# Moving three groups of SBUF tiles by 64 bytes in a four-layer graph network kernel

## What is computed

```python
h = relu(layernorm(x)); x = x + elu(softmax(where(adj > 0.5, leaky_relu(Wh1 + Wh2.T), -9e15), axis=1) @ (h @ W0))
h = relu(layernorm(x)); x = x + relu(D @ (adj + I) @ D @ h @ W1 + bias)      # D = diag(rsqrt(rowsum(adj + I)))
h = relu(layernorm(x)); x = x + relu(adj @ h @ W2) * row_mask
h = relu(layernorm(x)); x = x + relu(h @ Wa + ((adj @ h) / rowsum(adj)) @ Wb)
```

## The kernel before

| tiles | start modulo 512, before | after |
|---|---|---|
| w_hi, w_lo | 128 | 128 |
| v_rows, bias_rows, ident | 0 | 64 |
| xs, a_raw, a_hi, a_lo | 64 | 128 |
| a_rows, a_diag | 384 | 448 |
| h, h_hi, h_lo | 384 | 448 |
| t_hi, t_lo, ht_hi, ht_lo | 384 | 384 |
| z, act_out, scores, mask_add | 384 | 384 |
| p_hi, p_lo | 64 | 128 |

## Time and profile before

### The profile page before, as it was taken

How to read it: one execution, slowest core, us unless ns; L and a number is a source line. 1 busy time by engine, 2 the same in 40 slices (tenths; PEclk the granted TensorE clock), 3 DMA queues, 4 the chain that set the end, 5 groups by cost and what they waited for, 6 DMA issues and landing times.

```text
span 2565.7 us, 40515 instructions
## 1 busy us (share of the span) xinstructions
PE 2491.4 (97%) x13216; PEld 2151.6 (84%) x13216; DVE 2000.7 (78%) x4373; ACT 1398.7 (55%) x2571; POOL 1212.0 (47%) x1607
## 2 busy tenths in 40 slices
PE   2799999999999999999999999999999999999998
PEld 2688888888888888888888888888888888888887
DVE  6787887877877878788787787787787788788853
ACT  3555555555555555555555555556555555555542
POOL 2454545545544544544544544544544545445431
PEclk8899999999999999999999999999999999999999
DMA  4112122122122121122121221221221221221110
GB/s 143 42 38 59 50 58 58 47 61 56 49 62 51 53 62 50 55 62 49 55 62 48 56 62 48 57 62 47 57 62 46 59 62 45 59 63 45 43 34 25
DMA packets 338321, 141.35 MB, mean 55 GB/s; under 512 B 269760, under 2 KB 302528, under 8 KB 338112
## 3 DMA queue, kind: packets, MB, share of 16 engines
q1 hardware_dynamic: 338112, 138.75, 20.2%
HBM read 73.14 MB, written 33.55 MB: 42 GB/s over the span
## 4 chain that ended last, share of the span: by engine, by line
PE 95%; DVE 1%; issue 1%; POOL 1%; ACT 1%; SPq 0%; DMA 0%; POOLq 0%; ACTq 0%; DVEq 0%
PE O L314 46%; PE T L314 35%; PE X L314 13%; PE X L335 1%; POOL h_lo L802 0%; SPq L276 0%; ACT h L442 0%; DMA act_out<-w_all 0%; POOL xs L767 0%; DVE ht_lo L654 0%; DVE p_lo L633 0%; DVE scores L566 0%; DVE w_lo L556 0%; DVE ln_stats L584 0%; POOL ln_scale L788 0%
## 5 line engine op out<-in xcount | busy, mean ns | idle before, releaser
L802 POOL TENSOR_TENSOR h_lo<-h,h_hi 128x512 fp32r<-128x512 f32 x384 | 534.3, 1413 | 354.4 <-ACT h_hi L448 354.4
L442 ACT ACTIVATE h<-xs,ln_bias,ln_scale 128x512 f32<-128x512 f32 x512 | 396.0, 811 | 423.6 <-POOL ln_bias L796 423.6
L314 PE MATMUL O<-w_hi,t_hi 128*128 128x512 f32 x1536 | 597.8, 389 | 0.0
L314 PE MATMUL O<-w_lo,t_hi 128*128 128x512 f32 x1536 | 597.5, 389 | 0.0
L314 PE MATMUL O<-w_hi,t_lo 128*128 128x512 f32 x1536 | 597.5, 389 | 0.0
L639 DVE TENSOR_TENSOR t_lo<-T,t_hi 128x512 fp32r<-128x512 f32 x512 | 347.6, 689 | 297.1 <-ACT t_hi L454 297.1
L454 ACT CAST t_hi<-T 128x512 fp32r<-128x512 f32 x512 | 298.1, 583 | 417.7 <-PE T L314 417.7
L767 POOL TENSOR_TENSOR xs<-xs,act_out 128x512 f32<-128x512 f32 x128 | 164.0, 1300 | 591.1 <-ACT act_out L481 556.1
L584 DVE BATCH_NORM_STATS2 ln_stats<-xs 128x6 f32<-128x512 f32 x512 | 327.3, 679 | 18.3 <-POOL xs L773 12.5
L314 PEld LDWEIGHTS O<-w_hi,t_lo 128*128 128x128 f32 x1536 | 288.3, 188 | 59.8
L314 PEld LDWEIGHTS O<-w_hi,t_hi 128*128 128x128 f32 x1536 | 288.3, 188 | 55.3 <-DVE t_lo L639 0.5
(11 more groups left out here) (95 smaller groups left out, 5061.9 us busy)
## 6 DMA issues: line engine op xcount, KB each, us to landing
xs<-x SPq DMA_DIRECT2D x64, 512.0 KB, 3.6
out<-xs SPq DMA_DIRECT2D x64, 512.0 KB, 3.0
h<-act_out SPq DMA_DIRECT2D x976, 32.0 KB, 1.9
a_raw<-adj_t SPq DMA_DIRECT2D x64, 256.0 KB, 2.7
a_rows<-adj SPq DMA_DIRECT2D x64, 256.0 KB, 2.7
xs<-w_all SPq DMA_DIRECT2D x6, 512.0 KB, 6.9
act_out<-w_all SPq DMA_DIRECT2D x2, 512.0 KB, 6.6
z<-w_all SPq DMA_DIRECT2D x2, 512.0 KB, 6.4
```

The lines of the kernel that those rows point to most:

```text
L314: last = nc.tensor.matmul(psum, s, m, start=(start and n == 0 and i == 0), stop=(stop and n == len(pairs) - 1 and i == 2))
L442: nc.scalar.activation(h[:, k.odd, m], xs[:, k.xb, m], ACT.Relu, bias=ln_bias[:, k.quad, m:m + 1], scale=ln_scale[:, k.quad, m:m + 1], acc ...
L802: nc.gpsimd.tensor_tensor(h_lo[:, k.odd, m], h[:, k.odd, m], h_hi[:, k.odd, m].bitcast(F32), ALU.subtract).then_inc(h_lo_ready, 1)
```

## The change

A new tile `t_distance` of 448 bytes per partition is put ahead of t_hi, and the two unused tiles that exist grow by 64 bytes each. Everything from v_rows to h_lo lies 64 bytes further on, everything from t_hi to mask_add 512 bytes, and everything from p_hi on 576 bytes. The weights stay. Nothing reads or writes the three unused tiles, and no instruction of any engine differs but for its addresses.

```diff
-        distance = sb("distance", [P, 96])
+        distance = sb("distance", [P, 112])
...
         h_lo = sb("h_lo", [P, 2, NT, F], F32R)
+        t_distance = sb("t_distance", [P, 112])
         t_hi = sb("t_hi", [P, 2, FT, N], F32R)
...
-        p_distance = sb("p_distance", [P, 48])
+        p_distance = sb("p_distance", [P, 64])
         p_hi = sb("p_hi", [P, NT, N], F32R)
```

## The result

| | before | after |
|---|---|---|
| median of 20 runs each, us | 2567.18 | 2571.31 |
| lowest and highest | 2566.54, 2569.35 | 2569.17, 2572.74 |
| the profiled execution, us | 2567.61 | 2572.03 |
| its span, us | 2565.7 | 2570.2 |

After takes 1.0014 of the time before, interval [1.0008, 1.002]; the medians are 4.1 us apart. The forecast was 2565.0, a little less than before. The median lies inside the range 2546 to 2588, but the sign is the other one. The difference is under the 0.2% that the chances were set for, and yet its interval leaves out 1.

A forecast was written before the change was run, and what follows sets the result against it. The prediction took TensorE's matmul steps to bound the kernel; with only `gather_last` gaining 1.9 us and all else 0, 2566.7 became 2564.8, said as 2565.0 us, range 2546 to 2588.

The forecast's parts named there:

- What bounds the kernel: Steady part, about 2350 of 2566 us: TensorE always busy, so time is the number of matmuls times their step.
- Projections, 0 us: Matmuls with weights moving and t or ht loaded, 120 of 204 per period: offsets modulo 512 unchanged, so 0 us.
- Gathers, 0 us: 4608 matmuls of 256 columns: difference stays 320, step stays 117.6 ns; bounds 19.8 us less to 27.6 us more.
- The reading that the difference decides, and not the place: In the gathers: loaded less moving offset sets the step, so an unchanged difference of 320 costs 0 us.
- `gather_last`, 1.9 us less: 768 matmuls, t moving and a loaded: step falls from 229.2 to 226.7 ns; bounds nothing or 4.6 us.
- Edges between groups, 0 us with a bound of 1: Last matmul ahead of a gather, h loaded beside it: some 190 at 5 ns, under 1 us, taken as 0.
- Other engines and DMA, 0 us: Other engines not later, DMAs of `carry` hidden though their share might rise to at most twice 0.32; 0 us.
- The ht_lo that had 0.2 us in hand: Layer 3's turned h on VectorE: lateness might cost up to 12 us, expected 0; 0.23 together with the slower rival.
- Nothing happens: First rival: TensorE never waits on anyone, no address matters, 2566.7 us; chance 0.12.
- The boundary: Second rival: operands off a multiple of 128 bytes cost, not the difference; 2556.5 us, chance 0.27 with its variant.
- The third, slower one: Loaded operand 64 bytes past a multiple of 128 costs 2.5 to 6 ns per gather matmul; 0.23 with late ht_lo.
- the second rival's variant: Gathers all run at the start-up's 113.3 ns, 19.8 us less, 1.9 lost behind; 2547 us, within the rival's 0.27.

The follow-up runs named there:

- e3: Every tile 64 bytes further on than in the kernel before, weights and t included, so all differences stay; 1.0002 [0.9993, 1.0012] of its time.
- e8: Against the kernel before, a and p moved to offset 0 and h to 320 modulo 512, weights and t kept; 0.9989 [0.9978, 1.0001].
- e9: Against the kernel before, a and p moved to offset 192 and h to 256 modulo 512, weights and t kept; 1.0014 [1.0004, 1.0024].
- e12: The placement of e8 again with more rounds (a and p at 0, h at 320 modulo 512), against the kernel before; 0.9989 [0.998, 0.9998].
- e1: Against the kernel before, only the graph matrices a and the attention p moved 64 bytes on, h and t kept; 1.004 [1.0025, 1.0055].
- e4: Against the kernel before, a and p moved 128 bytes on and h 64, modulo 512, weights and t kept; 1.0068 [1.0053, 1.0083], 2585.5 us.
- e5: Against the kernel before, a moved to offset 0 and p to 448 modulo 512, the rest kept; 1.0058 [1.0035, 1.0081].
- e7: Against the kernel before, a moved to offset 256 and p to 192 modulo 512, the rest kept; 1.0051 [1.0029, 1.0074].
- e13: Against the kernel before, a and p moved to offset 0 and h to 224 modulo 512, weights and t kept; 1.0009 [0.9999, 1.0019], 2570.0 us.
- e11: Against the kernel before, a moved to offset 224 and p to 160 modulo 512, the rest kept; 1.0056 [1.0036, 1.0076].
- e14: Against the kernel before, a and p moved to offset 96 and h to 160 modulo 512, weights and t kept; 1.0058 [1.0039, 1.0076].
- e10: Against the kernel before, a moved to offset 32 and p to 96 modulo 512, the rest kept; 1.0046 [1.003, 1.0062].

## Why the prediction was wrong

**What bounds the kernel: right.** TensorE is busy for all of each period in after too, the waits are empty, and in the steady part the whole difference is matmuls that start later one after the other.

**Projections, 0 us: right within the group, wrong at its start.** From the sixth matmul on the step is 226.7 ns as before.

**Gathers, 0 us: right.** Extra 107 before and after. The reading that the difference decides, and not the place, is what e3 shows.

**`gather_last`, 1.9 us less: right.** 27.5 to 0 ns a graph is 1.8 us less for 64 graphs.

**Edges between groups, 0 us with a bound of 1: this is the step that failed.** It looked at one kind of edge only, the one that leads into a gather (weights or t moving, h loaded), and took for its price the 5 ns by which one slow step differs from a fast one. The edge that costs is the one out of a gather, and it costs five steps and not one: 27.5 ns, 3 x 64 = 192 times, 5.3 us. The forecast lies 6.3 us under the result: 5.3 are these edges, and 0.4 the median of before, 2567.18 over 20 runs for the 2566.74 that the forecast started from. The prediction had a row of that very kind before it and read it as small: in the start-up three projections behind a fast gather take 0.69 us where three take 0.68 elsewhere. It priced them at 0.01 us and let them occur only where the gathers ran fast. From that row it should have kept a term of 0.01 us for each of 192 edges, and by the rounding of both times up to 0.02, in the forecast itself: 1.9 to 3.8 us more, which takes away the gain of `gather_last` or turns the sign. That would still be under the 27.5 ns of each edge; no row that it shows has that size.

**Other engines and DMA, 0 us: right.** The ht_lo that had 0.2 us in hand never made TensorE wait. The DMA share of a period is 0.21 and 0.20 against 0.22 and 0.21, so that pieces crossing more boundaries, if they cost anything, stay hidden.

**The rivals.** "Nothing happens" is refuted by `gather_last` and the projections, which went opposite ways; that their sum is small is chance. The boundary is refuted by e3. The third, slower one had the sign, at 2576 to 2592 instead of 2571.3, but not the mechanism: its price was to fall on the 4608 gather matmuls, and they did not move. The fast gathers of the second rival's variant do exist, one in three, in e8, e9 and e12, but the best placement gains 40 ns a period and not the 72 x 4.3 = 310 of the variant.

**A premise that e1 corrected.** The prediction took 256 bytes between the operands for the free distance, from the projections. It is free for 512 columns (226.7 ns) and nearly the worst for 256: (2720 + 153) / 24 = 119.7 ns, against 117.8 at 320. One relation can't be carried from one shape to the other.

**What stays open.** What inside TensorE turns a difference of starts into a later step isn't shown. The profile has no row for its reads, and no run here takes the loading and the moving apart. The crossing and the pair at the gather's entrance are not told apart either, since t was never moved against the weights. Nor is it shown why the loss is largest at C 32, or what the 1.3 us outside the steady part are.

## What to carry to other kernels

In a kernel that is bound by TensorE from end to end, the start of an SBUF tile is worth up to 0.7% (e4 against before), so that it is worth measuring a few placements by time, and keeping all distances when tiles are added: moving everything alike costs nothing (e3). Choose for the sequence of groups, not for one group: the best one here (e12, 0.9989 [0.998, 0.9998]) makes `gather_last` worse and wins at the group behind it. And price the edges between groups in both directions from the list in order of time, since a mean by shape hides 27 ns in 5440.

## What the runs showed of the hardware

- The step of a float32r matmul depends on how the starts of its operands differ modulo 256 bytes; moving all of them, or two of them by 256, changes nothing (e3, e5 with e7). For 256 columns it is 116.7 to 120.1 ns in the slow way over eight differences (e13, e11), for 512 columns 226.7 (after) to 234 (`gather_last` in e11). With the same difference it still varies by up to 1.3 ns with what runs ahead (D 128 in e5: 125 and 156 in 24).
- One pair of tiles can run in two ways in the same kernel: a step of 113.8 ns behind `gather_last`, 117.8 behind a projection (e12). Which one is entered depends on what ran ahead, and so does what is lost behind: 25 or 10 ns in e9, 0 or 27 in e13.
- A change from one pair of tiles to another can cost 0 to 51 ns, spread over the first ten matmuls of the next group (27.5 in after, 51 in e14), and up to 10 in the last step ahead of a gather (e10), with no wait in the trace. The Trainium skill ("SBUF — State Buffer", Who interferes with whom) says that TensorE never waits on anyone. The trace agrees that no other engine comes into it (in after the waits are empty but for 0.6 us, and the other engines' busy times are within 3 us of before's), but not the reading in the prediction that no address matters by that: 1.0068 [1.0053, 1.0083] in e4 for the same instructions.
